# Graph attention over edge pairs: sorting products ahead of the previous pair's sums, denominators in the first keys' bank, maxima transposed four products earlier

## The reference, cut to what matters

```python
x_cat = concatenate([node_feat[src], node_feat[dst], edge_feat], axis=-1)
r = x_cat @ Wr.T + br
q = (node_feat @ Wq.T + bq).reshape(n, H, D)           # H = 8 heads of D = 64
k = (r @ Wk.T + bk).reshape(e, H, D)
v = (r @ Wv.T + bv).reshape(e, H, D)
a = einsum('ehd,ehd->eh', q[dst], k) * scaler
amax = segment_max(a, dst)                             # edges come sorted by dst
ae = exp(a - amax[dst])
asum = segment_sum(ae, dst)
out = segment_sum(v * (ae / asum[dst])[..., None], dst)
```

## Time and profile before

| | |
|---|---|
| median of 3 runs | 1941.12 us (1935.93 to 1944.87) |
| the profiled execution | 1957.55 us |
| its span, first to last instruction | 1955.8 us, mean granted clock of TensorE 0.932 |
| TensorE / DVE / ACT / POOL busy over the span | 85% / 65% / 53% / 38% |
| the loop over pairs, 365 to 1497 us | TensorE 1072.67 of 1132 us busy, granted clock 1.00 |

### The profile page before, as it was taken

The page is one execution under the profiler, slowest core; times in us unless marked ns, Lnnn a source line. Parts: engine busy times, 40 slices in busy tenths (PEclk is TensorE's granted clock), DMA queues, the critical chain, the costliest instruction groups (busy, mean ns, idle before and its releaser), DMA issues. The chain is left out here.

```text
span 1955.8 us, 25729 instructions
## 1 busy us (share of the span) xinstructions
PE 1662.3 (85%) x7160; PEld 1212.4 (62%) x7162; DVE 1273.3 (65%) x2943; ACT 1027.3 (53%) x3595; POOL 737.3 (38%) x727
## 2 busy tenths in 40 slices
PE   7978877999999999999999999999999467888723
PEld 6756656777777777777777777777776233443411
DVE  6764443777777777777777777777776354432588
ACT  3871111677667776776677667766776233310011
POOL 0101112455555555555555555555554000000033
PEclk9988888999999999999999999999999688999955
DMA  5860004666656666666666666666663423100001
GB/s 172 308 264 33 34 35 134 191 187 208 198 182 193 199 206 191 193 206 196 193 193 204 205 193 193 208 201 193 193 200 121 169 83 124 61 0 1 22 11 42
DMA packets 127102, 300.20 MB, mean 153 GB/s; under 512 B 29088, under 2 KB 50727, under 8 KB 126962
## 3 DMA queue, kind: packets, MB, share of 16 engines
q0 software_dynamic: 66224, 190.99, 28.3%
q1 hardware_dynamic: 60738, 107.59, 19.0%
HBM read 271.40 MB, written 66.58 MB: 173 GB/s over the span
## 5 line engine op out<-in xcount | busy, mean ns | idle before, releaser
L1115 ACT ACTIVATE wv<-vv,expd 128x64 f32<-128x64 f32 x1256 | 316.8, 334 | 3.2 <-ACT expd L1105 0.7
L1127 ACT ACTIVATE old<-old,expd 128x64 f32<-128x64 f32 x1256 | 307.7, 333 | 0.0
L1065 POOL DMA_INDIRECT merge<-new,put_id x157 | 159.8, 1018 | 381.3 <-DVE new L1249 352.4
L1296 PE MATMUL psV<-M_hi,efT_hi 128*128 128x512 f32 x628 | 266.1, 424 | 0.0
L1296 PE MATMUL psK<-M_hi,efT_hi 128*128 128x512 f32 x628 | 250.1, 398 | 6.5 <-ACT efT_hi L1090 6.5
L1297 PE MATMUL psV<-M_lo,efT_hi 128*128 128x512 f32 x628 | 249.8, 398 | 0.0
L1297 PE MATMUL psK<-M_lo,efT_hi 128*128 128x512 f32 x628 | 249.4, 397 | 0.0
L1036 POOL DMA_INDIRECT old<-merge,dst_id x157 | 195.8, 1247 | 49.1 <-issue 47.5
L1302 PE MATMUL psV<-M_hi,efT_lo 128*128 128x512 f32 x628 | 192.1, 407 | 0.0
L1199 DVE TENSOR_TENSOR vv<-psV,kv 128x512 f32<-128x512 f32 x157 | 108.5, 691 | 121.4 <-remote 115.8
L1036 POOL DMA_INDIRECT kv<-kv_table,src_id x157 | 155.0, 987 | 85.5 <-issue 46.9
(11 more groups left out here) (261 smaller groups left out, 3200.9 us busy)
## 6 DMA issues: line engine op xcount, KB each, us to landing
efT<-in_ef_turned_dram SPq DMA_DIRECT2D x78, 512.0 KB
merge<-empty POOLq DMA_DIRECT2D x4, 2640.0 KB, 15.0
rows<-merge SPq DMA_DIRECT2D x40, 264.0 KB, 3.7
row_block<-dst_rows POOLq DMA_DIRECT2D x13, 768.0 KB, 7.1
dst_line<-dst_rows SPq DMA_DIRECT2D x78, 128.0 KB
end_line<-end_rows SPq DMA_DIRECT2D x78, 128.0 KB
kv_table<-kv_out SPq DMA_DIRECT2D x10, 512.0 KB, 5.6
raw<-in_L_gnn_Wr_dram SPq DMA_DIRECT2D x12, 256.0 KB, 5.1
```

Source lines behind the costliest of these rows:

```text
L1065: pool.indirect_dma_start(out=merge[2 * (p % 2) + u][:, :], out_offset=bass.IndirectOffsetOnAxis(ap=put_id[:, t:t + 1], axis=0), in_=new[p ...
L1115: act.activation(wv[:, u, h * DH:(h + 1) * DH], vv[:, u, h * DH:(h + 1) * DH], ACT.Copy, scale=expd[p % 2][:, u, 0, h:h + 1]).then_inc(wv_ ...
L1127: act.activation(rows, rows, ACT.Copy, scale=expd[p % 2][:, u, 1, h:h + 1]).then_inc(old_scaled, 1)
L1296: pe.matmul(out[:, :], efT_hi[b][:, u, c, :], Me_hi[:, c, col:col + D], start=c == 0, stop=False)
```

## The change

Three pieces move, and two waits with them.

- On TensorE `sort_scores(p)` stands in front of `sums(p - 1)`. In `sums`, the denominators of both tiles come first, ahead of the `psS` products.
- The denominators move from `psO`, which they shared with the sorted scores, to the first 16 columns of `psK[0]`. The keys of the next pair's first tile must therefore wait for `den_ready`, and the denominators for `k_added` of tile 2p (of the current pair).
- Inside the values of tile 2p + 1, `turn_runs` is called before the third matmul instead of the seventh, and `spread_top` before the seventh instead of the eleventh.
- On DVE `scan(p)` comes ahead of `scale_den(p - 1)` and `add_v(2p)`, and `merge_rows` adds the denominators ahead of the rows.

```diff
-        den = psO[:, 2 * P:2 * P + 2 * H].rearrange("p (u h) -> p u h", h=H)
+        den = psK[0][:, 0:2 * H].rearrange("p (u h) -> p u h", h=H)
...
                     dve.wait_ge(summed, t + 1)
+                    if u == 0:
+                        dve.wait_ge(den_scaled, p + 1)
+                        dve.tensor_tensor(new[b][:, 0:n, D:ROW], den[:, 0:n, :], old_den[:, 0:n, :],
+                                          ALU.add).then_inc(den_ready, 1)
                     dve.wait_ge(old_scaled, H * (t + 1))
...
-                dve.wait_ge(den_scaled, p + 1)
-                dve.tensor_tensor(new[b][:, 0:n, D:ROW], den[:, 0:n, :], old_den[:, 0:n, :], ALU.add).then_inc(den_ready, 1)
...
                     low_part(p + 1)
+                if here:
+                    scan(p)
                 if p >= 1:
                     scale_den(p - 1)
                 if both:
                     add_v(2 * p)
-                if here:
-                    scan(p)
...
                 for c in range(C):
+                    if c == 1:
+                        half_way()
                     if c == 3:
-                        half_way()
+                        near_end()
...
-                    if c == 2:
-                        near_end()
...
+                if t >= 4 and t % 2 == 0:
+                    pe.wait_ge(den_ready, t // 2 - 1)
                 product(psK[t % 2], t, 0, nothing, nothing).then_inc(k_done, 1)
...
-                if p >= 1:
-                    pe.wait_ge(den_ready, p)
+                pe.wait_ge(k_added, min(2 * p + 3, ET))
+                for u in range(tiles_of(p)):
+                    pe.matmul(den[:, u, :], same[p % 2][:, u, :].bitcast(F32), expd[p % 2][:, u, 0, :], start=True, stop=True)
...
-                    pe.matmul(den[:, u, :], same[p % 2][:, u, :].bitcast(F32), expd[p % 2][:, u, 0, :], start=True, stop=True)
...
+                if p < PAIRS:
+                    sort_scores(p)
                 if p >= 1:
                     sums(p - 1)
                 if p < PAIRS:
-                    sort_scores(p)
                     values(2 * p + tiles_of(p) - 1, lambda: turn_runs(p), lambda: spread_top(p))
```

## The result

| | before | changed |
|---|---|---|
| median | 1939.3 us (1935.93 to 1944.87, 4 runs) | 2062.85 us (2038.03 to 2081.53, 4 runs) |
| ratio | | 1.0551 (95% interval 1.0511 to 1.0592) |
| profiled execution | 1957.55 us, clock 0.932 | 2056.31 us, clock 0.894 |

Two of the four executions of the changed kernel, 2069.38 and 2081.53 us, are left out of the ratio as disturbed. The change made the kernel 5.5% slower; I had forecast 1875 us.

What follows compares the result with a forecast made beforehand. TensorE's own work was taken to bound the kernel. Closing the transposes' gap, -69.2 us, plus 3 us for sorting first made -66 us, taken off the median 1941.12 us: 1875 us, range 1858 to 1985 us.

Steps and rivals of the forecast that it cites:

- The gap: TensorE idle at the transposes until DVE's scan; earlier scan and earlier transposes close it, worth 69.2 us.
- Grouped denominators: Denominators side by side in TensorE's sums: could save or cost part of a switch, taken as 0.
- the covered waits for `den_ready` and `k_added`: Moved waits cost nothing: some 2.5 us of other products cover the next keys' wait; `k_added` is already met.
- The price of sorting first: Sorting products on TensorE may wait 0.17 us for the second score, 13 us at most in all; taken as 3 us.
- The fourth rival: Late second keys' add on DVE stalls TensorE's sort: 2045 us, or 1960 us if in half the pairs; chance 0.20.
- Subtracting from the median: Profiled execution 0.8% above the median 1941.12 us; the same 66 us taken off the median, giving 1875 us.
- No effect: Scan stays late through another DVE wait, transposes stop TensorE as long: within 0.5% of 1941 us; chance 0.13.
- the third: TensorE's report late by its own phase, some 2.9 us behind the values wherever the sort stands: 1965 us; chance 0.07.
- The first: Late report follows POOL's store; the loop from store to store sets a 14.6 us period: 1914 us; chance 0.15.

Runs made afterwards that it cites:

- the two runs with the reports in time: Changed kernel with the gathers of `old` from pair 2 on left out, 1894.43 us, or replaced by plain transfers of the same size, 1895.63 us.
- the kernel with both waits and late transposes: Changed kernel with stores behind the pair's values, `old` gathered behind the sorting products, transposes and spreading products back at seventh and eleventh matmul: 2046.48 us.

## Why the prediction was wrong

**The gap (right).** The scan follows `efT_lo`, the transposes' idle time is gone, and in the two runs with the reports in time the loop is 67 us shorter. Grouped denominators at 0 and the covered waits for `den_ready` and `k_added` held too, as far as the total shows: in the two windows shown of those runs TensorE is idle for 0.2 us at most, in 1065.

**The price of sorting first (the step that failed).** The sum gave it 3 us ("they may wait 0.17 us"). It was read in a pair whose keys were through 5.9 us behind the store. I had worked out that after the change they would be through 7.0 to 7.7 us behind it, and let one `kk` of the kernel before, which started at 7.5 us without waiting, speak against a delay. It is the wrong witness. Its train was slow: the first gather of `old` came 8.6 us behind the store (564.61 less 555.99), and in the changed kernel, too, `kk` at 7.44 passes with that gather at 8.5. The pair with the keys through at 6.7 was the right witness: its train ran without a pause, with that gather at 7.7 (578.69 less 570.98), and so it is in the late pairs of the changed kernel, with the keys through at 7.9 and `kk` held until 11.5. Rows 5 leave these gathers out:

```profile
564.61 1.16 POOL L1036 DMA_INDIRECT old<-merge,dst_id  x1 [0.30 <-issue]
...
578.69 0.95 POOL L1036 DMA_INDIRECT old<-merge,dst_id  x1 [0.30 <-issue]
```

The prediction asked only how far the keys are behind the store. That distance it had about right, 7.4 or 7.9 us in the two pairs shown. What it priced at 3 us came to 86.4 us of idle time before the sorting products, and to the clock behind it.

**The fourth rival (what happened, chance 0.20).** Place and mechanism were right, but that its 2045 us came near the 2063 us measured is luck, for the parts of that price were not. It took 2.27 us in every pair, 175 us in all. In fact `kk` is late in 29 pairs, by up to 3.8 us, TensorE then stands idle for up to 2.9 us before the sort, 84 us in the whole loop, and the granted clock then mostly drops to 0.50 for some 6 us. The clock was no term anywhere in the prediction, although it is worth nearly as much as the idle time: 75 us more busy time for the same instructions. The run that let `kk` wait but kept the sums ahead (29 waits, clock 1.00, ratio 1.0001) bears out that the stop of TensorE makes the cost, though its waits are shorter, too (53.7 us in all, not 94.3). That the clock falls because of the stop is read from the order of rows, here and in the table's last column: from 365 to 1450 us the trace of the changed kernel has 25 stretches at 0.50, and each begins between 0.2 us before and 2.0 us after the end of a stop of TensorE of 2.6 to 2.7 us; six of its 31 stops of over 1 us bring none. No run changes the clock alone. (The rival's price for half of the pairs was also a little off: by its own periods it is +0.22 x 77, not +0.25 x 77.)

**Subtracting from the median (a second, smaller slip).** With the gap wholly closed the runs took 1894 and 1896 us, not 1875. The profiled execution of before was 0.8% above the median, and I let the forecast inherit that offset. But TensorE's own work is a floor: 1957.55 - 66 = 1892 us would have been right. That the extra 16 us of the profiled execution were gap, too, fits this; no second profile of before shows it.

**The other rivals.** No effect is refuted by the result, in which the transposes' wait is gone; the third (lateness by TensorE's own phase) by the runs without `old`'s gathers. The first, lateness that follows the store, was the right cause with the wrong consequence: it moves with POOL's train behind the store, but sets no loop of its own here; what it costs depends on which report falls into it.

## What to carry to other kernels

A wait that is harmless where it stands is a property of the moment, not of the instruction: before moving work on TensorE, ask which reports will then arrive while another engine's train of gathers runs, as a wait like that shows, and what stands right behind them in the queue. If POOL issues gathers back to back there, move the gathers (one semaphore wait turned 2063 us into 1918 us here) rather than the products. Count a stop of TensorE of some 3 us twice, once for itself and once for the clock behind it, and take a forecast that closes all idle time as absolute work, not as a difference from a median.

## What the runs showed of the hardware

- While POOL issues its train of two stores and six gathers without a pause, semaphore reports of TensorE reach DVE late: keys through 7.9 us behind the store were seen at 11.5 us. With the last two gathers left out, replaced by plain transfers of the same size, or held back, the same report comes by 8.7 us. Gathers that fetch almost nothing delay it all the same. In the 25 pairs of the changed kernel (365 to 1450 us) whose keys were through at 8.8 to 11.5 us they were seen at once, and the first gather of `old` was issued at 8.6 us or later, as where POOL had stopped for 2.48 us inside its train.
- After 2.73 us without work TensorE's granted clock is at 0.50 for at least 5.8 us of the following work, beginning some 2 us after it resumed (from 1030.43 to about 1032.5, where the products still start 0.22 to 0.28 apart).
- In the kernel with both waits and late transposes, the rows of a gather were used no sooner than 4.3 us after its issue where the maximum waited for them (365 to 1450 us), though the gather's row on POOL is 0.95 us long.
